# Long attention on one Trainium2 core: weighted sum in full fp32 on two column halves of TensorE, row sums by additions

## The chip, the cores and the metric

One core of a Trainium2 chip runs the whole program; the other seven are idle. The metric is the device time of one execution in microseconds. Three timed runs of the kernel before gave 3176.74, 3182.2 and 3185.15 us (median 3182.2).

Engines: PE is TensorE (matmuls; PEld is its load of the stationary operand), DVE is VectorE, ACT is ScalarE, POOL is GpSimd, and SP issues the DMAs.

## The reference

Four layers, each a cross attention of 896 queries (16 batches of 56) on a context, and a feed-forward part. The change touches the attention of layers 1, 2 and 3 ("long": 1500 keys per batch, 16 heads that share keys and values of width 64). With the weights folded, a batch computes for its 896 query rows (16 heads x 56)

```
scores = q @ k.T                     # 896 x 1500, contraction 64
attn   = softmax(scores, axis=-1)
ctx_c  = attn @ kv_rope              # 896 x 64, contraction 1500
out    = (fold of ctx_c over heads) @ B
```

`kv_rope` is the context with a rotary embedding, the same in the three layers. Layer 0 attends to the first 56 keys only ("short").

## The kernel before

**Precision.** An fp32r operand is read with reduced precision, in one pass of PE; an fp32 operand is multiplied in full. The kernel before splits both factors of each product into a high and a low fp32r part and adds three products (high x high, high x low, low x high).

**Short attention (`attend_short`, layer 0)** runs 8 steps of two batches and, beside it, `Rotation` makes the rotated context: `sines` on POOL, `cosines` and `sums` on DVE give `cr`; `value_highs` (ACT) and `value_lows` (DVE) split it into `vs`, which `store` writes to `kvn` in DRAM with extra columns (a column of ones at index 64, so that the weighted sum also gives the row sums). `turn`, `turned_highs` and `turned_lows` do the same for the transposed copy (`kvt_hi`, `kvt_lo`). Its DMAs are issued in order by SP: `load` of the next pair of batches, then `store` of an earlier one.

**Long attention (`attend_long`)** takes the 16 batches in turn. All engines run a program order written out by hand, unrolled over four batches. A batch has 12 units. A unit is two chunks of 125 keys against one half of the query rows (448 of 896): units 0 to 5 are the first query half, 6 to 11 the second.

- PE, per unit u: `scores` of unit u+2 (4 matmuls of 448 columns into banks 0 to 3, L1013); a `top_scores` piece (L1026, one matmul of 500 columns for the row maxima of the next batches, banks 6 and 7 in turns; 21 pieces per batch); `weigh_high` of unit u (4 matmuls, L1043: stationary `v` of 125 x 66, high and low part, moving `hi`); a second top piece; `weigh_low` (2 matmuls, L1050). They gather in bank 4 (first half) or 5 (second half). At u=7 `turn` (L1031) transposes the maxima. Units 0 to 6 and 8 to 10 have two pieces, unit 11 one, unit 7 none.
- ACT, per unit: two exponentials of the same scores, one to `raw` in fp32 (L1136), one to `hi` in fp32r (L1139).
- DVE, per unit: `tops` (L1083, the maximum of each piece) and `low` (L1095: `raw` minus `hi`).
- The row sums come as row 64 of the weighted sum. ACT copies it with the numerators (`cu`, L1145); SP sends it to DRAM and back across 128 partitions (`sums`), DVE inverts it (L1100), SP sends it to DRAM and back as 64 equal rows (`scales`), and POOL multiplies (`place`, L1184).
- SP, per batch: wait for the end of the last batch, then the loads of `qm`, `kl`, `v` (from `kvn`, 125 partitions x 6336 bytes) for the next batch, of `kh` and `q` for the one after, a wait until these have landed, `sums`, `shifts`, `scales`.

`project_out` (L1210) and the folding of weights (`fold_latent`, L414 and L432; `rotated_queries` of layer 2, L588 and L601) are not touched; they matter here because they multiply in full fp32. L1210 and L432 fill all 128 columns of PE. L414 and L601 use 64: L414 writes in turns to partitions 0 to 63 and 64 to 127 of a bank, L601 writes four records in a row to the same half. One full fp32 matmul is two MATMUL records in the trace.

Of the kernel before, what the change touches and what calls it, by code (L numbers as in the profile page):

```python
# [13 lines left out]
FP32 = mybir.dt.float32  # L14
# [23 lines left out]
DV = D + 2  # L38
HH = NH // 2
UNITS = 12  # L40
# [110 lines left out]
class Rotation:  # L151
# [6 lines left out]
    def __init__(self, G, st):  # L158
# [4 lines left out]
        self.vs = st.sb("vs", [KP, 2, NC, 2, DV], F32R)  # L163
        self.hi, self.lo = st.sb("hi", [128, L], F32R), st.sb("lo", [128, L], F32R)
        self.out_n, self.out_t = G["kvn_out"], G["kvt_out"]
        self.extra, self.tables = st.sem("extra"), st.sem("tables")
        self.in_n = [st.sem(f"in_n{u}") for u in range(2)]
        self.sin_n, self.cos_n, self.sum_n, self.hi_n, self.lo_n, self.turned, self.hi_t, self.lo_t = (
            st.sem(n) for n in ("sin_n", "cos_n", "sum_n", "hi_n", "lo_n", "turned", "hi_t", "lo_t"))
# [11 lines left out]
    def store(self, sp, m):  # L181
        sp.wait_ge(self.lo_n, m + 1)
        sp.dma_start(self.G["kvn"][bass.ds(m * 2, 2)].rearrange("b p n -> p b n"),
                     self.vs[:].rearrange("p b c h d -> p b (c h d)").bitcast(FP32)).then_inc(self.out_n, 16)
# [5 lines left out]
    def extra_columns(self, pool):  # L190

        parts = self.vs[:, :, :, :, :].rearrange("p b c h d -> p (b c) h d").bitcast(FP32)
        pool.memset(parts[:, :, 0, D:D + 1], 1.0).then_inc(self.extra, 1)
        pool.memset(parts[:, :, 0, D + 1:DV], 0.0).then_inc(self.extra, 1)
        pool.memset(parts[:, :, 1, D:DV], 0.0).then_inc(self.extra, 1)

# [12 lines left out]
    def sums(self, dve, m, u, first):  # L209

        dve.wait_ge(self.cos_n, m + 1)
        if not first:
            dve.wait_ge(self.turned, 3 * m)
        cn, cm = (v.rearrange("p b (c e d) -> p c b e d", e=2, d=D // 2) for v in (self.cn[:, u], self.cm[:]))
# [3 lines left out]

    def value_highs(self, act, m, first):
        if first:  # L220
            act.wait_ge(self.extra, 3)
        else:
            act.wait_ge(self.out_n, 16 * m)
        act.wait_ge(self.sum_n, 2 * m + 2)
        act.activation(self.vs[:, :, :, 0, 0:D], self.cr[:].rearrange("p c b d -> p b c d"),
                       ACT.Copy).then_inc(self.hi_n, 1)

    def value_lows(self, dve, m):
        dve.wait_ge(self.hi_n, m + 1)
        dve.tensor_tensor(self.vs[:, :, :, 1, 0:D], self.cr[:].rearrange("p c b d -> p b c d"),  # L230
                          self.vs[:, :, :, 0, 0:D].bitcast(FP32), ALU.subtract).then_inc(self.lo_n, 1)
# [428 lines left out]
def attend_short(nc, G, q_all, ctxT):  # L660
# [6 lines left out]
    with Stage(nc, "att0") as st:  # L667
# [22 lines left out]
        with nc.Block() as block:  # L690

            @block.sync
            def _(sp):
# [4 lines left out]
                def step(i, m, u, first, fresh):  # L698
                    rot.load(sp, m, u, fresh)
                    if not fresh:  # L700
                        rot.store(sp, m - 2)

                pairs(sp, step)
                for u in range(2):
                    rot.store(sp, LAST - 1 + u)
# [60 lines left out]
            def _(dve):  # L766
# [3 lines left out]
                def step(i, m, u, first, fresh):  # L770
# [11 lines left out]
                    if not first:  # L782
                        rot.value_lows(dve, m - 1)
# [22 lines left out]
                rot.value_lows(dve, LAST)  # L806
# [4 lines left out]
            def _(act):  # L811
                def step(i, m, u, first, fresh):
# [16 lines left out]
                    rot.value_highs(act, m, first)  # L829
# [6 lines left out]
            def _(pool):  # L836
                pool.memset(oc[:, :, NT, :], 0.0).then_inc(pad_done, 1)
                pool.memset(pw[:, :, NT * S:], 0.0).then_inc(pad_done, 1)
                rot.extra_columns(pool)
# [34 lines left out]
def attend_long(nc, G, l, ctxT):  # L874
# [5 lines left out]

    PS = G["PS"]
    with Stage(nc, f"att{l}") as st:
        kh, kl = st.sb("kh", [128, 4, L], F32R), st.sb("kl", [D + 1, 2, L], F32R)
        v = st.sb("v", [KP, 2, NC, 2, DV], F32R)
        q, qm = st.sb("q", [128, 4, NH * S], F32R), st.sb("qm", [D + 1, 2, NH * S], F32R)
        raw = st.sb("raw", [KP, 3, 2, HALF])
        hi, lo = st.sb("hi", [KP, 3, 2, HALF], F32R), st.sb("lo", [KP, 3, 2, HALF], F32R)
        top, nm = st.sb("top", [128, 2, NT, NS]), st.sb("nm", [128, 2, NT])
        nmh = st.sb("nmh", [NT, 2, 128], F32R)
        cu, rsb = st.sb("cu", [D + 1, 4, HALF]), st.sb("rsb", [D, 2, T])  # L890
# [889 lines left out]
```

## Time and profile before

| | us |
|---|---|
| median of three runs | 3182.2 |
| profiled execution, its own time | 3180.73 |
| its span | 3178.9 |
| PE busy | 2781.7 (88%) |
| DVE busy | 1970.7 (62%) |
| ACT busy | 1531.7 (48%) |
| POOL busy | 470.6 (15%) |

The mean granted clock of TensorE is 0.886 of 2.4 GHz; a granted clock of 0.50 is its level of 1.2 GHz. Long attention takes three stretches of some 500 us each, with other stages between (about 682 to 1194, 1452 to 1961 and 2385 to 2884 us in the profile). A row of the page's part 5 has the line, engine, operation, output<-input, shapes and count, then busy us and mean ns of one, then idle us before it and who ended them. Matmuls are pipelined: a record lasts longer than the distance to the next, so it is distances between starts, and not lengths, that add up to time on PE.

### The profile page before, as it was taken

How to read it: one execution, taken by the hardware profiler on the slowest of the kernel's cores; microseconds unless marked ns; L12 is line 12 of the kernel's file. 1: busy time of each engine (PE TensorE's matmuls, PEld its weight loads, DVE VectorE, ACT ScalarE, POOL GpSimd, SP SyncE). 2: the span in 40 equal slices, each digit the busy share in tenths (PEclk: the TensorE clock that was granted, in tenths of full speed). 3: DMA queues.
4: the chain of work that ended last, by engine and by line, in shares of the span. 5: the costliest groups of instructions: out<-in, count | busy, mean ns of one | idle time of the engine just before them, and what ended most of it. 6: DMA issues, size and time to landing. Idle time of an engine off the chain costs nothing. (4 is left out here: it accounts for less than half of the span.)

```text
span 3178.9 us, 38552 instructions
## 1 busy us (share of the span) xinstructions
PE 2781.7 (88%) x12773; PEld 2205.7 (69%) x12773; DVE 1970.7 (62%) x3007; ACT 1531.7 (48%) x2192; POOL 470.6 (15%) x350
## 2 busy tenths in 40 slices
PE   6777299779999985997999998699879999995798
PEld 4676199747777764654777776599757777774698
DVE  3563244258888864566888883344347888873444
ACT  3332144237777761213777774344226677771343
POOL 0221033000101110350010111133100010110232
PEclk9556599769999996997999999799868999997899
DMA  1333144363434412013443430233443443420343
GB/s 42 117 152 124 36 110 117 109 169 76 100 86 105 100 40 94 17 54 105 106 95 87 108 92 12 72 118 118 131 141 82 96 98 85 108 61 8 106 117 94
DMA packets 108025, 293.22 MB, mean 92 GB/s; under 512 B 24025, under 2 KB 49577, under 8 KB 106588
## 3 DMA queue, kind: packets, MB, share of 16 engines
q1 hardware_dynamic: 107900, 291.62, 34.6%
q8 instruction: 70, 1.15, 0.2%
q14 instruction: 55, 0.45, 0.0%
HBM read 241.90 MB, written 49.51 MB: 92 GB/s over the span
## 5 line engine op out<-in xcount | busy, mean ns | idle before, releaser
L1083 DVE TENSOR_REDUCE att_top<-banks 128x1 f32<-128x500 f32 x1008 | 670.9, 674 | 223.1 <-PE banks L1026 217.7
L1095 DVE TENSOR_TENSOR att_lo<-att_raw,att_hi 125x896 fp32r<-125x896 f32 x576 | 648.2, 1125 | 51.0 <-ACT att_hi L1139 48.0
L1136 ACT ACTIVATE att_raw<-banks 125x896 f32<-125x896 f32 x576 | 527.7, 916 | 306.6 <-PE banks L1013 302.1
L1043 PE MATMUL banks<-att_hi,att_v 125*66 125x448 f32 x2304 | 564.8, 367 | 0.0
L1139 ACT ACTIVATE att_hi<-banks 125x896 fp32r<-125x896 f32 x576 | 525.8, 913 | 0.0
L1395 PE MATMUL banks<-moe_xs,moe_w 128*128 128x448 f32 x2040 | 446.7, 369 | 69.4 <-DVE moe_xs L1510 67.2
L1026 PE MATMUL banks<-att_kh,att_q 128*128 128x500 f32 x1008 | 420.0, 424 | 55.6 <-DMA att_q<-q_rows 46.2
L1395 PEld LDWEIGHTS banks<-moe_xs,moe_w 128*128 128x128 f32 x2040 | 387.3, 190 | 103.0 <-DVE moe_xs L1510 68.7
L1043 PEld LDWEIGHTS banks<-att_hi,att_v 125*66 125x66 f32 x2304 | 317.2, 138 | 137.2 <-issue 0.4
L1184 POOL TENSOR_TENSOR ctx_ctxT<-att_cu,att_rsb 64x448 f32<-64x448 f32 x96 | 142.7, 1486 | 1408.9 <-DMA att_rsb<-rs_rows 1405.1
L1013 PE MATMUL banks<-att_q,att_kh 128*125 128x448 f32 x1152 | 333.6, 371 | 1.0 <-ACT att_hi L1139 1.0
L1050 PE MATMUL banks<-att_lo,att_v 125*66 125x448 f32 x1152 | 332.9, 370 | 0.0
L1013 PE MATMUL banks<-att_qm,att_kl 65*125 65x448 f32 x1152 | 332.2, 369 | 0.0
L1478 POOL TENSOR_TENSOR moe_sc<-moe_sg,moe_cb 128x448 f32<-128x448 f32 x170 | 196.1, 1153 | 683.2 <-ACT moe_sg L1452 683.2
L1500 DVE TENSOR_TENSOR moe_hf<-banks,moe_sc 128x448 f32<-128x448 f32 x170 | 106.2, 625 | 306.4 <-POOL moe_sc L1478 306.4
L1026 PEld LDWEIGHTS banks<-att_kh,att_q 128*128 128x128 f32 x1008 | 197.8, 197 | 133.8 <-DMA att_q<-q_rows 47.7
L1013 PEld LDWEIGHTS banks<-att_q,att_kh 128*125 128x125 f32 x1152 | 217.5, 189 | 52.9 <-ACT att_hi L1139 2.8
L1408 PE MATMUL banks<-moe_h,moe_w 128*128 128x448 f32 x1020 | 234.2, 366 | 4.1 <-DVE moe_h L1505 4.1
L1013 PEld LDWEIGHTS banks<-att_qm,att_kl 65*125 65x125 f32 x1152 | 217.4, 189 | 21.9
L1408 PEld LDWEIGHTS banks<-moe_h,moe_w 128*128 128x128 f32 x1020 | 191.4, 188 | 20.2 <-DVE moe_h L1505 5.2
L1050 PEld LDWEIGHTS banks<-att_lo,att_v 125*66 125x66 f32 x1152 | 155.8, 138 | 67.9 <-issue 10.4
L1460 ACT ACTIVATE moe_h<-moe_hf 128x448 fp32r<-128x448 f32 x170 | 98.5, 580 | 195.0 <-DVE moe_hf L1500 195.0
(182 smaller groups left out, 2484.2 us busy)
## 6 DMA issues: line engine op xcount, KB each, us to landing
moe_cb<-comb_rows SPq DMA_DIRECT2D x85, 448.0 KB
att_v<-kvn SPq DMA_DIRECT2D x48, 773.4 KB
att_kh<-kvt_hi SPq DMA_DIRECT2D x96, 375.0 KB, 8.4
moe_raw<-L_experts_dram SPq DMA_DIRECT2D x85, 384.0 KB, 6.1
q_rows<-mats_q SPq DMA_DIRECT2D x24, 896.0 KB
att_q<-q_rows SPq DMA_DIRECT2D x48, 448.0 KB, 16.0
att_kl<-kvt_lo SPq DMA_DIRECT2D x48, 375.0 KB, 5.5
kvn<-att_vs SPq DMA_DIRECT2D x8, 1546.9 KB
```

Source lines behind the costliest of these rows:

```text
L1013: last = pe.matmul(PS[2 * (u % 2) + c % 2][0:KP, 0:HALF], k[:, KP * c:KP * c + KP], rhs[:, HALF * e:HALF * e + HALF], start=part == 0, sto ...
L1026: pe.matmul(PS[6 + (PIECES * s + n) % 2][:, 0:SB], q[:, s, 128 * t:128 * t + 128], kh[:, s, SB * c:SB * c + SB], start=True, stop=True).th ...
L1043: pe.matmul(PS[4 + e][0:DV, 0:HALF], v[:, s % 2, c, part, :], hi[:, u % 3, c % 2, :], start=c == part == 0, stop=False)
L1050: last = pe.matmul(PS[4 + e][0:DV, 0:HALF], v[:, s % 2, c, 0, :], lo[:, u % 3, c % 2, :], start=False, stop=c == NC - 1)
L1083: dve.tensor_reduce(top[:, s % 2, n // NS, n % NS:n % NS + 1], PS[6 + (PIECES * s + n) % 2][:, 0:SB], AX.X, ALU.max).then_inc(mx_done, 1)
L1095: dve.tensor_tensor(lo[:, u % 3], raw[:, u % 3], hi[:, u % 3].bitcast(FP32), ALU.subtract).then_inc(dve_low, 1)
L1136: act.activation(raw[:, u % 3], scored, ACT.Exp).then_inc(exp_done, 1)
L1139: act.activation(hi[:, u % 3], scored, ACT.Exp).then_inc(hi_done, 1)
L1184: pool.tensor_tensor(ctxT[64 * e:64 * e + 64, :, b * S:b * S + S], a, r, ALU.mult).then_inc(placed, 1)
L1395: last = pe.matmul(PS[2 * e + m][:, 0:HALF], w[:, s, pw, o:o + 128], xs[:, px, k, HALF * e:HALF * e + HALF], start=n == 0, stop=n == 3 * K ...
L1408: last = pe.matmul(PS[4 + 2 * d + e][:, 0:HALF], w[:, s, pw, o:o + 128], h[:, s, ph, e, :], start=start and n == 0, stop=stop and n == 2)
L1478: pool.tensor_tensor(sc[:, e, :], sg[:, e, :], cb[:, s, HALF * e:HALF * e + HALF], ALU.mult).then_inc(comb_done, 1)
```

## The change

- Values are kept whole: `Rotation` stores `cr` itself to `kvn` (`store_values`, 64 floats per key, no extra columns, runs of 256 bytes); `value_highs`, `value_lows` and the memsets go. `sums` now waits for the store of the step before. In `attend_long`, `v` is 125 partitions x 3072 bytes.
- A unit is one chunk of 125 keys against both query halves. Its four `scores` matmuls are the same in number and size.
- ACT makes one exponential per unit, in fp32, into a ring of four (`ex`).
- `weigh` replaces `weigh_high` and `weigh_low`: two full fp32 matmuls per unit, stationary `v` of 125 x 64, the first query half into partitions 0 to 63 of a bank, the second into 64 to 127.
- Row sums: DVE adds two units (`pair`, six per batch), POOL adds the pairs up (`gather`, five per batch of 125 x 896), and at unit 3 of the next batch PE multiplies the result by a column of ones: 7 full fp32 matmuls (`sums`) with a stationary operand of 128 columns that lie 7 floats apart, into the bank of the top pieces. DVE inverts from PSUM. The top piece number 13, the next in that bank, waits for the inverse.
- SP has no `sums` any more; `scales` goes ahead of `shifts` and loads two halves of 64 partitions. `place` is one multiplication of 128 x 448.

```diff
@@ PE
-                def weigh_high(s, b, u): ...   # 4 matmuls fp32r, v 66 columns, moving hi
-                def weigh_low(s, b, u): ...    # 2 matmuls fp32r, moving lo
+                def weigh(s, b, u):
+                    pe.wait_ge(exp_done, UNITS * b + u + 1)
...
+                    for e in range(2):
+                        last = pe.matmul(PS[4 + s % 2][64 * e:64 * e + 64, 0:HALF], v[:, s % 2, u, :],
+                                         ex[:, u % RING, e, :], start=u == 0, stop=u == UNITS - 1)
+                    last.then_inc(pv_done, 1)
+                def sums(s, b, tops):
+                    pe.wait_ge(gathered, GATHERS * b + GATHERS)
+                    pe.wait_ge(mx_done, tops)
+                    for t in range(NT):
+                        last = pe.matmul(sums_bank(s)[:, t:t + 1], acc[:, (s + 1) % 2, t:T:NT], one[:, :],
+                                         start=True, stop=True)
+                    last.then_inc(sums_ready, 1)
@@ top_scores
+                    if n == SUMS_PIECE and not known(b, 2):
+                        pe.wait_ge(inverted, b - 1)
@@ batch on PE, unit u
+                        if u == SUMS_AT and not known(b, 1):
+                            sums(s, b - 1, PIECES * b + PIECES + (SUMS_PIECE - 1 if left else 0))
@@ DVE
-                def low(b, u): ...
+                def pair(b, p):
+                    dve.wait_ge(exp_done, UNITS * b + 2 * p + 2)
...
+                    dve.tensor_tensor(two[:, p % 3, :], ex[:, a].rearrange("p e n -> p (e n)"),
+                                      ex[:, a + 1].rearrange("p e n -> p (e n)"), ALU.add).then_inc(paired, 1)
@@ ACT
+                        act.wait_ge(pv_done, UNITS * b + u - RING + 1)
+                        act.wait_ge(paired, PAIRS * b + (u - RING) // 2 + 1)
...
+                    act.activation(ex[:, u % RING], scored, ACT.Exp).then_inc(exp_done, 1)
@@ POOL
+                    pool.tensor_tensor(a, two[:, 0, :] if n == 1 else a, two[:, n % 3, :], ALU.add).then_inc(gathered, 1)
...
+                    pool.tensor_tensor(ctxT[:, :, b * S:b * S + S], c, r, ALU.mult).then_inc(placed, 1)
@@ Rotation
+    def store_values(self, sp, m):
+        sp.wait_ge(self.sum_n, 2 * m + 2)
+        sp.dma_start(self.G["kvn"][bass.ds(m * 2, 2)].rearrange("b p (c d) -> p c b d", c=NC), self.cr[:]
+                     ).then_inc(self.out_n, 16)
```

## Rows read from the trace of the kernel before

**Rows 1.** The page's part 5, three groups of long attention (columns above).

```profile
L1083 DVE TENSOR_REDUCE att_top<-banks 128x1 f32<-128x500 f32 x1008 | 670.9, 674 | 223.1 <-PE banks L1026 217.7
L1095 DVE TENSOR_TENSOR att_lo<-att_raw,att_hi 125x896 fp32r<-125x896 f32 x576 | 648.2, 1125 | 51.0 <-ACT att_hi L1139 48.0
L1136 ACT ACTIVATE att_raw<-banks 125x896 f32<-125x896 f32 x576 | 527.7, 916 | 306.6 <-PE banks L1013 302.1
```

**Rows 2.** Windows of two batches: length, each engine's busy us (records), clock, DMA.

```profile
756.60:786.40 29.80, 29.80 (x144) 22.80 (x143) 25.98 (x36) 21.64 (x28) 3.04 (x2) 1.00 0.41 92
2502.00:2535.40 33.40, 31.64 (x145) 23.72 (x144) 26.29 (x36) 21.68 (x29) 2.83 (x2) 0.95 0.40 92
```

**Rows 3.** Timeline of PE, units 7 and 8 of a batch: start, length, what.

```profile
849.18 0.97 PE L1043 MATMUL banks<-att_hi,att_v 125*66 125x448 f32 x4
850.08 0.38 PE L1031 MATMUL banks<-ident,att_nm 128*7 128x128 f32 x2
850.39 0.62 PE L1050 MATMUL banks<-att_lo,att_v 125*66 125x448 f32 x2
850.85 0.58 PE L1013 MATMUL banks<-att_q,att_kh 128*125 128x448 f32 x2
...
853.35 0.57 PE L1013 MATMUL banks<-att_q,att_kh 128*125 128x448 f32 x2
```

**Rows 4.** Timeline of PE, queries of layer 2 (64 columns, one half).

```profile
1307.14 1.72 PE L601 MATMUL banks<-q_tc,mats_N 96*64 96x448 f32 x4
1308.79 2.68 PE L588 MATMUL banks<-q_xs,mats_Q 128*96 128x448 f32 x12
1311.39 1.72 PE L601 MATMUL banks<-q_tc,mats_N 96*64 96x448 f32 x4
```

**Rows 5.** Timeline of DVE, folding: copies, each after four heads of L414.

```profile
616.46 0.69 DVE L472 COPY keep_B<-banks 128x512 f32<-128x512 f32 x1 [0.17 <-PE banks L414]
617.33 0.69 DVE L472 COPY keep_B<-banks 128x512 f32<-128x512 f32 x1 [0.17 <-PE banks L414]
```

**Rows 6.** Windows of L414, L1210 and L432 alone: length, PE (records), PEld, clock, DMA.

```profile
615.37:617.10 1.73, 1.73 (x18) 0.98 (x14) 1.00 0.00 0
1200.05:1206.05 6.00, 6.00 (x29) 5.29 (x28) 1.00 0.00 0
617.30:619.00 1.70, 1.70 (x16) 1.70 (x17) 1.00 0.00 0
```

**Rows 7.** Timeline: a handover from DVE to PE.

```profile
701.98 0.67 DVE L1083 TENSOR_REDUCE att_top<-banks 128x1 f32<-128x500 f32 x1
702.70 0.28 PEld L1026 LDWEIGHTS banks<-att_kh,att_q 128*128 128x128 f32 x1 [0.30 <-DVE att_top L1083]
```

**Rows 8.** Timelines of ACT, DVE and POOL: end of layer 3's attention.

```profile
2870.74 0.54 ACT L1145 ACTIVATE att_cu<-banks 65x448 f32<-65x448 f32 x1 [1.92 <-PE banks L1050]
2876.43 0.20 DVE L1100 RECIPROCAL att_rout<-att_rin 128x7 f32<-128x7 f32 x1 [6.31 <-DMA att_rin<-rs_rows]
2881.42 2.32 POOL L1184 TENSOR_TENSOR ctx_ctxT<-att_cu,att_rsb 64x448 f32<-64x448 f32 x2 [4.05 <-DMA att_rsb<-rs_rows]
```

**Rows 9.** One line's durations, ns: min/median/max.

```profile
L1095 DVE TENSOR_TENSOR att_lo<-att_raw,att_hi x576: 1073/1081/2067, 709.4 to 2868.9; 125x896 fp32r<-125x896 f32 x192
L1184 POOL TENSOR_TENSOR ctx_ctxT<-att_cu,att_rsb x96: 1120/1157/2030, 774.9 to 2882.6; 64x448 f32<-64x448 f32 x96
L657 POOL TENSOR_TENSOR q_tc<-q_tc,q_ts x32: 2072/2117/2123, 1304.6 to 1432.9; 96x896 f32<-96x896 f32 x32
```

**Rows 10.** Timeline of SP, two steps of short attention.

```profile
179.83 0.58 SPq L178 DMA_DIRECT2D att_cn<-ctxN_dram  x1
...
205.75 0.36 SPq L178 DMA_DIRECT2D att_cn<-ctxN_dram  x1
```

**Rows 11.** Windows while `kvn` is stored, and while `q_rows` is (896-byte runs).

```profile
191.00:202.00 11.00, 11.00 (x53) 10.88 (x54) 2.17 (x4) 0.83 (x2) 0.00 (x0) 0.50 0.32 130
651.00:673.00 22.00, 16.91 (x46) 8.20 (x44) 16.19 (x26) 12.94 (x25) 0.00 (x0) 0.93 0.97 311
```

More of the change, by code:

```diff
@@ L699, in step @@
                     rot.load(sp, m, u, fresh)
+                    if not first:
+                        rot.store_values(sp, m - 1)
                     if not fresh:
-                        rot.store(sp, m - 2)
+                        rot.store_turned(sp, m - 2)
                 pairs(sp, step)
+                rot.store_values(sp, LAST)
                 for u in range(2):
-                    rot.store(sp, LAST - 1 + u)
+                    rot.store_turned(sp, LAST - 1 + u)
             @block.tensor
@@ L992, in _ @@
                     if b:
-                        sums(b - 1)
+                        scales(b - 1)
                     if b < B - 1:
                         shifts(b + 1)
-                    if b:
-                        scales(b - 1)
-                sums(B - 1)
                 scales(B - 1)
@@ L1010, in scores @@
                             pe.wait_ge(m_in[s % 2], of_two(s, b, 16))
-                        for c in (2 * j, 2 * j + 1):
+                        for e in range(2):
                             k, rhs = (kh[:, s, :], q[:, s, :]) if part == 0 else (kl[:, s % 2, :], qm[:, s % 2, :])
-                            last = pe.matmul(PS[2 * (u % 2) + c % 2][0:KP, 0:HALF], k[:, KP * c:KP * c + KP],
+                            last = pe.matmul(PS[2 * (u % 2) + e][0:KP, 0:HALF], k[:, KP * u:KP * u + KP],
                                              rhs[:, HALF * e:HALF * e + HALF], start=part == 0, stop=part == 1)
@@ L1076, in _ @@
                 scores(0, 0, 1)
+                pe.wait_ge(ones, 2)
                 emit(pe, batch)
+                pe.wait_ge(inverted, B - 1)
+                sums(0, B - 1, PIECES * B)
             @block.vector
@@ L1114, in batch @@
                             shift((s + 1) % 4, b + 1)
-                        if u == 10 and not known(b, 1):
-                            invert(s + 1, b - 1)
                 for n in range(PIECES):
@@ L1174, in _, with gather @@
                 pool.memset(kl[D:D + 1, :, :].bitcast(FP32), 1.0).then_inc(ones, 1)
+                pool.wait_ge(ones, 1)
+                pool.memset(one[:, :], 1.0).then_inc(ones, 1)
+                def gather(b, n):
+                    a = acc[:, b % 2, :]
+                    pool.wait_ge(paired, PAIRS * b + n + 1)
+                    if n == 1 and b >= 2:
+                        pool.wait_ge(sums_ready, b - 1)
+                    if n > 1:
+                        pool.wait_ge(gathered, GATHERS * b + n - 1)
+                    pool.tensor_tensor(a, two[:, 0, :] if n == 1 else a, two[:, n % 3, :], ALU.add).then_inc(gathered, 1)
                 def place(b):
                     s = b % 2
[L1180 to L1189 removed]
+                    pool.wait_ge(rs_in[s], b // 2 * 32 + 32)
+                    pool.wait_ge(cu_done, b + 1)
+                    c, r = (m[:, s, :].rearrange("p (h s) -> p h s", s=S) for m in (cu, rsb))
+                    pool.tensor_tensor(ctxT[:, :, b * S:b * S + S], c, r, ALU.mult).then_inc(placed, 1)
+                pool.wait_ge(ones, 2)
+                for b in range(B):
+                    for n in range(1, PAIRS):
+                        gather(b, n)
+                        if n == 3 and b:
+                            place(b - 1)
+                place(B - 1)
 def project_out(nc, G, l, Bm, ctxT):
```

179 lines of the change are left out of this document (59 added, 120 removed).

## The prediction, made blind

> **What bounds the kernel now.** I read the page's shares first, then windows of single batches of long attention, then the timeline of PE inside one batch, and last the few places elsewhere in the trace where full fp32 matmuls run. The page has PE at 88% of the span. In a batch of long attention it is everything: 29.80 us of 29.80 at granted clock 1.00 (2.4 GHz), while DVE has 25.98, ACT 21.64 and POOL 3.04 [rows 2]. So long attention, 48 batches of 29.8 us or 1430 of 3179 us, is a queue of PE records, and the change has to be judged by the length of that queue. DVE is the second: a top piece costs 0.67 and a `low` 1.13 us, 576 of them; one exponential costs ACT 0.92 [rows 1]. A unit with two top pieces takes 2.50 us (850.85 to 853.35) [rows 3].
>
> A batch holds 120 fp32r records of 448 columns, 21 of 500 and the turn. The turn adds 0.45 us: from 849.18 to 850.85 there are four records of L1043, the turn and two of L1050 in 1.67 us, six at 0.204 make 1.22 [rows 3]. 29.35 us over 64,260 columns are 0.457 ns per column, so 0.205 us for a record of 448.
>
> **The weighted sum.** Removed are six records per unit: 1.23 us. Added are two full fp32 matmuls, which are four records. Their pace without halves: L1210 runs 28 to 29 records of 256 columns in 6.00 us at clock 1.00, 0.21 us each or 0.84 ns per column, and a matmul is two [rows 6]. With 448 columns a record takes 0.376 us. If the four ran one after another they would take 1.50 us and the change would lose. The halves decide.
>
> L414 shows them. It alternates between partitions 0 to 63 and 64 to 127; a copy on DVE waits for each four heads, that is for eight records of 256 columns. Two such waits end 0.87 us apart (616.46 and 617.33, DVE idle and waiting for PE both times) [rows 5], at granted clock 1.00 [rows 6]. That is 0.108 us per record, half of L1210's. Its order, two records for one half and then two for the other, is the new unit's. So a unit's four records fill two slots: 2 x 0.376 = 0.75 us.
>
> What PE pays to go from full-width records to 64-column ones and back: L601 (64 columns, 448 moving, four records, all to one half, so no overlap) starts at 1307.14, and the next full-width record at 1308.79: 1.65 us against 4 x 0.376 = 1.50, so 0.15 more. The twelve L588 records after it take 2.60 against 12 x 0.205 = 2.46, 0.14 more [rows 4]. A round trip is 0.29 us. The turn gives a lower value: L1031 starts 0.08 late, L1050 0.09 after its two records of 128 columns (0.22) should have ended, and the next 0.05 late, 0.22 us in all [rows 3]. I take 0.29, since L601 has the new records' shape; 0.22 is the lower bound, and 0.34 the upper (0.05 more, if the second half's first load also shows). The new unit spends 0.75 + 0.29 = 1.04 us in place of 1.23: 0.19 saved, times 576 = **-107 us** (-147 to -78).
>
> **Row sums on PE.** 7 matmuls, 14 records with one moving column, so their load of 128 stationary columns sets the pace. L432 (128 columns, 64 moving) runs 15 to 16 records in 1.70 us at clock 1.00: 0.11 us each [rows 6]. 14 x 0.11 = 1.54 us, 48 times = **+74 us**. No record of before has a stationary operand with a step of 7 floats; bounds are 0.106 (the same row) and 0.21 (half its pace), so +71 to +141. A gain is excluded: PE has no idle time in a batch to hide them [rows 2].
>
> **The wait for the inverse.** After `sums` the order has top piece 13, which waits for DVE. What PE loses: the last record's end lies about 0.16 after the next one could start (500-column top pieces last 0.39 and follow at 0.23; I take the difference), a handover of 0.05 (DVE ends at 702.65, PE's load starts at 702.70) [rows 7] twice, the reciprocal 0.20 [rows 8]. 0.46 us, of which nothing is covered, because S, W and the rest stand behind the waiting piece on PE's queue; 45 batches (the last of each layer is in the tail): **+20 us** (+13 to +36, when DVE is still in a top piece).
>
> **Small terms.** The turn now follows a 64-column record and precedes a full one, so it shares that record's way back: 0.31 in place of 0.45, at most -6 us, I take **-3**. One batch took 33.40 us with PE idle 1.8 us and the clock at 0.95 [rows 2], waiting for the load of `q`; that load stands behind `v`, which falls from 6336 to 3072 bytes per partition. `v` uses few DMA engines, as the store of `kvn` from the same 125 partitions does (share 0.32, 130 GB/s) [rows 11], so this stall goes: **-4** (0 to -6).
>
> **DVE, ACT, POOL in a batch.** DVE has two top pieces per unit and one `pair` per two units: 21 x 0.67 + 6 x 1.1 = 20.7 of 29 us, was 26. ACT 12 x 0.92 + 0.5 = 11.5. POOL five adds of 125 x 896, 2.12 us each by L657, and one multiplication of 448, 1.16: 12 us [rows 9]. None is near PE. `gather` follows its `pair` at once and the next `pair` is two units, 4.6 us, later, so they hardly meet. The last `gather` ends some 4 us after unit 11 starts, `sums` comes 9 us after. SP's `scales` moves ahead of `shifts`: it takes over the 2 to 3 us in which `sums` waited for its DMA, and the row that scores of the next batch need at unit 10 is as early as before. Cost: nothing.
>
> **Tails.** Before, from the last weighted sum (2870.74) to the end of `place` (2881.42 + 2.32): 13.0 us [rows 8]. Now `pair` and `gather` follow the last exponential, so `sums` starts about 1.4 us after the last `weigh`; then 0.2, from the reciprocal to `place` 4.99 [rows 8], `place` 1.16 [rows 9]: 7.8 without `sums` (counted above). 5.2 saved, three times: **-16 us** (-8 to -20).
>
> **Short attention.** A step takes 25.9 us (179.83 to 205.75) [rows 10]. What goes on ACT and DVE (3.6 us per step) lies beside PE and stays hidden: zero, at best -5. The store of `kvn` moves to the front of the queue and ahead of the next load, with 3000 runs of 256 bytes. Its bytes are half (768 KB at 130 GB/s: 6 us); if each run costs what a run of 896 bytes costs (311 GB/s over 16 engines: 0.046 us) and it too uses 5 engines, 600 x 0.046 = 28 us [rows 11]. The two copies of `kvt` and the load behind it need some 10 us more (2.25 MB, at the two rates of rows 11). Below 16 us the step is not touched; at 28 it grows by 12, seven times: +84. I take a run at 0.024, 14 us, and **+3** (-5 to +84).
>
> The Trainium skill (SBUF — State Buffer, the part on Door 1: the DMA port swizzle) says that SBUF is read in lines of 16 bytes and that each access that crosses to a new line pays; with a step of 28 bytes every column of `sums` does. No row here shows such a load, and the rows on L432 have contiguous columns. By the rule the price is that of the first rival below.
>
> **Sum.** -107 + 74 + 20 - 3 - 4 - 16 + 3 = -33 from the profiled execution's own 3180.7 us: 3148; that execution is 1.5 us under the median of the runs, so **3149 us**.
>
> **Rivals.** (A) *The strided load halves the pace of `sums`.* 0.21 in place of 0.11 per record, 14 x 48 times: +67, 3216 us, slower than before. It decides from 0.16 per record on (-33 + 34). For: every load in the trace that keeps 0.11 is contiguous. Against: nothing in the trace. (B) *The halves don't overlap in so short a burst.* Between two full-width records four records might need three slots: +0.376 x 576 = +217, 3366 us. Against: L414's groups show two slots per two matmuls, but in a run of 16. (C) *The short runs stretch short attention:* +72 more than I took, 3220 us. (D) *Smaller passage and quick handovers:* 0.22 per round trip and 0.3 us per wait, -40 and -7: 3102 us. (E) *Collisions of DVE and POOL:* L1095 has a maximum of 2067 ns against a median of 1081, L1184 2030 against 1157 [rows 9], so an operation doubles when the two meet. If each `pair` met a `gather`, two units would take DVE 4 x 0.67 + 2.07 = 4.75 us against PE's 4.63: +0.12, five times per batch, 48 batches: +29, 3178 us, no change.
>
> **Chances.** Forecast 0.53, A 0.14, B 0.04, C 0.08, D 0.14, E 0.07. The forecast's own range is 3115 to 3185 (the passage -40 to +29, the wait -7 to +16, the rest within 10). A measurement of this kernel tells about 0.3%, 9.5 us, from no change: faster is below 3172.7, slower above 3191.7. Of the forecast's 0.53 I put 0.47 below, 0.05 within and 0.01 above; D is faster, E within; A splits 0.02 below, 0.02 within, 0.10 above, C 0.02 below, 0.01 within, 0.05 above, B above. Faster 0.65, same 0.15, slower 0.20. The range that holds 8 in 10 is 3105 to 3230.
>
> **What would show it.** Right: in a batch of the changed kernel PE is still busy all the time at clock 1.00, a batch takes about 29.5 us (29.8 - 2.3 + 1.5 + 0.5 - 0.1); the four records of `weigh` start within 0.38 us (two slots), and `scores` behind them 1.04 us after the first; `sums` takes 1.5 us and one gap of 0.5 follows; the tail is near 9.3 us. Wrong: `weigh` records one by one at 0.376; `sums` near 3 us; DVE or POOL named as what PE waits for; steps of short attention above 26 us, waiting for `kvn`.

## The result, and the profile after

The changed kernel takes 3377.3 us (median of 4 runs, 3372.09 to 3386.32), the kernel before, run beside it, 3179.5: ratio 1.063 with a 95% interval of [1.0611, 1.0649], so 6.3% slower. The forecast was 3149 us with a range of 3105 to 3230. The profiled execution has a span of 3373.4 us and a mean granted clock of 0.845, where before had 3178.9 and 0.886.

Lines have moved: L1083 is now L1060 (top pieces on DVE), L1136 is L1115 (exponential), L1026 is L999 (top pieces on PE), L1013 is L984 (`scores`), L1184 is L1168 (`place`). L1014 is `weigh`, L1023 the row sums, L1075 `pair`, L1161 `gather`, L1082 the reciprocal. From the page's shares and its part 5:

```profile
PE 2971.3 (88%) x12293; PEld 2014.0 (60%) x12293; DVE 1685.5 (50%) x2711; ACT 1041.4 (31%) x1560; POOL 889.5 (26%) x542
...
L1060 DVE TENSOR_REDUCE att_top<-banks 128x1 f32<-128x500 f32 x1008 | 679.5, 677 | 524.9 <-PE banks L999 510.0
L1115 ACT ACTIVATE att_ex<-banks 125x896 f32<-125x896 f32 x576 | 528.2, 917 | 1058.8 <-PE banks L984 1058.8
L1161 POOL TENSOR_TENSOR att_acc<-att_acc,att_two 125x896 f32<-125x896 f32 x192 | 405.4, 2111 | 537.6 <-DVE att_two L1075 537.1
L1075 DVE TENSOR_TENSOR att_two<-att_ex 125x896 f32<-125x896 f32 x288 | 320.9, 1116 | 60.7 <-ACT att_ex L1115 60.0
```

DVE, ACT and POOL did what the prediction said: the operations of before kept their length (L1060 677 ns against 674 [rows 1]), DVE and ACT got lighter, and both wait for PE longer. PE's busy time grew by 190 us (2781.7 to 2971.3). So the loss is on PE. Its timeline in units 2 and 3 of a batch (start, length, engine, line, what, count, idle before):

```profile
851.60 0.97 PE L1014 MATMUL banks<-att_ex,att_v 125*64 125x448 f32 x4
852.50 0.49 PE L999 MATMUL banks<-att_kh,att_q 128*128 128x500 f32 x1
852.84 0.57 PE L984 MATMUL banks<-att_q,att_kh 128*125 128x448 f32 x2
853.25 0.57 PE L984 MATMUL banks<-att_qm,att_kl 65*125 65x448 f32 x2
853.66 3.18 PE L1023 MATMUL banks<-att_one,att_acc 125*128 125x1 f32 x14
857.34 0.47 PE L999 MATMUL banks<-att_kh,att_q 128*128 128x500 f32 x1 [0.50 <-DVE att_rout L1082]
857.74 0.97 PE L1014 MATMUL banks<-att_ex,att_v 125*64 125x448 f32 x4
858.64 0.79 PE L999 MATMUL banks<-att_kh,att_q 128*128 128x500 f32 x1
859.22 0.95 PE L984 MATMUL banks<-att_q,att_kh 128*125 128x448 f32 x2
```

Two things are to be seen. From the first record of the row sums (853.66) to top piece 13 (857.34) PE spends 3.68 us; the prediction had 1.54 + 0.46 = 2.0. And from 858.6 the same instructions take longer: two records of `scores` last 0.95 us where they lasted 0.57 six us earlier. The windows say why (length, PE busy and records, PEld, DVE, ACT, POOL, granted clock, DMA share, GB/s); the first two are whole batches, the third the stretch of the row sums, the fourth what follows:

```profile
801.86:835.16 33.30, 32.91 (x135) 18.46 (x134) 20.34 (x29) 11.71 (x14) 11.61 (x6) 0.95 0.34 74
835.16:870.06 34.90, 34.40 (x134) 19.33 (x133) 20.29 (x29) 11.71 (x14) 11.60 (x6) 0.90 0.32 71
851.20:857.30 6.10, 5.64 (x26) 4.42 (x24) 1.97 (x4) 1.83 (x2) 0.00 (x0) 1.00 0.90 173
857.30:864.10 6.80, 6.76 (x18) 3.51 (x19) 3.30 (x5) 0.92 (x1) 2.09 (x1) 0.60 0.16 50
```

Behind each stretch of row sums the granted clock falls from 1.00 to 0.50 (2.4 to 1.2 GHz) for 3.4 to 10.2 us; such a time at 0.50 is called a fall here. Counted in each layer from 35 us behind the first weighted sum to the last, the kernel before was at 0.50 for 3.4 us in the three layers together, the changed one for 304. Of 42 batches 26 last 33.3 us (3.4 us at 0.50), three 34.4 to 34.9 and 13 35.8 us (10.2 us at 0.50), in place of 29.8 [rows 2].

### The profile page after: what moved, and what is told of

It reads as the page before. It is cut to its first block and busy times, and to the rows that moved or that the text cites. A ratio compares the mean times of both kernels' runs of the same rounds, so it can differ in the third digit from the quotient of the medians.

```text
span 3373.4 us, 36689 instructions
## 1 busy us (share of the span) xinstructions
PE 2971.3 (88%) x12293; PEld 2014.0 (60%) x12293; DVE 1685.5 (50%) x2711; ACT 1041.4 (31%) x1560; POOL 889.5 (26%) x542
## 5 line engine op out<-in xcount | busy, mean ns | idle before, releaser
L1060 DVE TENSOR_REDUCE att_top<-banks 128x1 f32<-128x500 f32 x1008 | 679.5, 677 | 524.9 <-PE banks L999 510.0
L1115 ACT ACTIVATE att_ex<-banks 125x896 f32<-125x896 f32 x576 | 528.2, 917 | 1058.8 <-PE banks L984 1058.8
L1014 PE MATMUL banks<-att_ex,att_v 125*64 125x448 f32 x2304 | 614.5, 615 | 0.0
L999 PE MATMUL banks<-att_kh,att_q 128*128 128x500 f32 x1008 | 496.2, 500 | 70.8 <-DMA att_q<-q_rows 42.7
L1161 POOL TENSOR_TENSOR att_acc<-att_acc,att_two 125x896 f32<-125x896 f32 x192 | 405.4, 2111 | 537.6 <-DVE att_two L1075 537.1
L999 PEld LDWEIGHTS banks<-att_kh,att_q 128*128 128x128 f32 x1008 | 211.2, 210 | 463.3 <-DVE att_top L1060 384.5
L984 PE MATMUL banks<-att_q,att_kh 128*125 128x448 f32 x1152 | 373.1, 408 | 0.0
L984 PE MATMUL banks<-att_qm,att_kl 65*125 65x448 f32 x1152 | 357.7, 394 | 0.0
L1075 DVE TENSOR_TENSOR att_two<-att_ex 125x896 f32<-125x896 f32 x288 | 320.9, 1116 | 60.7 <-ACT att_ex L1115 60.0
L984 PEld LDWEIGHTS banks<-att_q,att_kh 128*125 128x125 f32 x1152 | 226.6, 206 | 99.6 <-ACT att_ex L1115 42.1
L1161 POOL TENSOR_TENSOR att_acc<-att_two 125x896 f32<-125x896 f32 x48 | 102.7, 2140 | 620.5 <-DVE att_two L1075 620.5
L984 PEld LDWEIGHTS banks<-att_qm,att_kl 65*125 65x125 f32 x1152 | 238.0, 207 | 25.8
L1014 PEld LDWEIGHTS banks<-att_ex,att_v 125*64 125x64 f32 x2304 | 122.3, 144 | 202.9 <-issue 202.6
L1395 PEld LDWEIGHTS banks<-moe_h,moe_w 128*128 128x128 f32 x1020 | 191.4, 188 | 20.3 <-DVE moe_h L1492 5.2
L1023 PEld LDWEIGHTS banks<-att_one,att_acc 125*128 125x128 f32 x672 | 158.4, 324 | 6.2 <-issue 5.5
L1023 PE MATMUL banks<-att_one,att_acc 125*128 125x1 f32 x672 | 153.2, 356 | 2.9 <-issue 2.9
```

The source lines that it names most:

```text
L984: last = pe.matmul(PS[2 * (u % 2) + e][0:KP, 0:HALF], k[:, KP * u:KP * u + KP], rhs[:, HALF * e:HALF * e + HALF], start=part == 0, stop=pa ...
L999: pe.matmul(PS[6 + (PIECES * s + n) % 2][:, 0:SB], q[:, s, 128 * t:128 * t + 128], kh[:, s, SB * c:SB * c + SB], start=True, stop=True).th ...
L1014: last = pe.matmul(PS[4 + s % 2][64 * e:64 * e + 64, 0:HALF], v[:, s % 2, u, :], ex[:, u % RING, e, :], start=u == 0, stop=u == UNITS - 1)
L1023: last = pe.matmul(sums_bank(s)[:, t:t + 1], acc[:, (s + 1) % 2, t:T:NT], one[:, :], start=True, stop=True)
L1060: dve.tensor_reduce(top[:, s % 2, n // NS, n % NS:n % NS + 1], PS[6 + (PIECES * s + n) % 2][:, 0:SB], AX.X, ALU.max).then_inc(mx_done, 1)
L1075: dve.tensor_tensor(two[:, p % 3, :], ex[:, a].rearrange("p e n -> p (e n)"), ex[:, a + 1].rearrange("p e n -> p (e n)"), ALU.add).then_in ...
```

## The experiments

A batch is measured as the distance between two of DVE's L1065 reductions (one per batch, the shift); the first of the 15 distances of a layer is left out, so there are 42. Each ratio is taken to runs of the kernel before that were made beside the kernel; their medians were 3172.6 to 3181.1 us. A batch counts in the last column if some of it is at 0.50. Where a text written ahead of a run speaks of 14 one-column matmuls, these are the 14 records of seven matmuls.

| kernel | median us | ratio to before, 95% | batch at clock 1.00 | batches with falls |
|---|---|---|---|---|
| after | 3377.3 | 1.063 [1.0611, 1.0649] | none seen | 42 of 42 |
| e1_together | 3225.7 | 1.0151 [1.0117, 1.0186] | 30.24 | 19 |
| e2_wide_moving | 3306.6 | 1.0399 [1.0367, 1.0432] | 31.88 | 28 |
| e3_no_row_sums | 3076.8 | 0.9677 [0.9651, 0.9704] | 28.09 | 0 |
| e4_other_bank | 3371.3 | 1.0611 [1.0581, 1.064] | 31.22 (one) | 41 |
| e5_ones_stationary | 3122.7 | 0.9826 [0.9813, 0.984] | 28.83 | 0 |
| e6_together_other_bank | 3168.5 | 0.9972 [0.996, 0.9985] | 29.64 | 4 |
| e7_values_between | 3073.0 | 0.9669 [0.9654, 0.9684] | 28.09 | 0 |
| e8_same_half | 3504.7 | 1.1034 [1.1017, 1.1051] | 37.03 | 0 |
| e9_spread | 3490.4 | 1.0972 [1.0948, 1.0996] | none steady | 39 |
| e10_standing | 3356.9 | 1.0564 [1.0547, 1.0581] | none | 42 |
| e12_spread_shifts_first | 3205.3 | 1.0105 [1.0084, 1.0126] | 30.58 | 0 |
| e11_both | 3112.5 | 0.9795 [0.978, 0.981] | 28.82 | 1 |

A fall of 3.4 us costs a batch 1.5 us (e1_together: medians 30.24, 31.79 and 33.24 us with none, one and two times 3.4 us at 0.50). The experiments e3_no_row_sums, e7_values_between, e8_same_half and e10_standing leave out row sums, and e1_together and e6_together_other_bank mix them up: only their time counts.

**e1_together: contiguous loads.** `sums` takes `acc[:, (s + 1) % 2, 128 * t:128 * t + 128]` in place of `t:T:NT`, so each row is divided by another row's sum.

> The changed kernel, but each of the seven row-sum matmuls loads 128 columns that lie together in place of 128 with a step of 7 floats; so each query row is divided by another row's sum (left wrong: only the time counts). Stride theory: the records of the row sums follow at 0.11 us as contiguous fp32 loads do, not 0.23, so 14 x 0.12 = 1.7 us less per batch, -80 us. Rival (the pace comes from the form with one moving column, whatever the step): 0.23 stays, no change, 3377 us. On the clock: if the granted clock falls because PE stands in the row sums too long, the stretch is now 2.4 us in place of 4.1 and the low stretches (about 100 us per layer) shrink; then up to another 95 us go, 3200 us. If it falls for another reason, about 3295 us.

The records of L1023 now start 0.112 us apart (median), in after 0.230. From the first to the next top piece it is 2.10 us, at its end a wait for the inverse:

```profile
877.91 1.62 PE L1023 MATMUL banks<-att_one,att_acc 125*128 125x1 f32 x14
880.01 0.46 PE L999 MATMUL banks<-att_kh,att_q 128*128 128x500 f32 x1 [0.48 <-DVE att_rout L1082]
```

The price of the predicted term, 2.0 us, holds for contiguous columns; the stride of 28 bytes adds 1.6 us per batch. And of 42 batches with falls 19 are left.

**e2_wide_moving: 64 ones instead of one.** `one` is [KP, 64] and each matmul writes 64 equal columns.

> The changed kernel, but the moving operand of the row-sum matmuls is 64 equal columns of ones in place of one; DVE inverts every 64th. Result as before. Step, number of records and the wait for the inverse stay. Clock theory (the granted clock falls in every batch because PE moves almost no columns during the row sums): the low stretches go or shrink, a batch loses up to 2 us, 3377 - 95 = 3282 us, with the records still at 0.23 us. Rival (the clock falls because of the wait after the row sums, or by itself in this mix of half-width and full-width records): low stretches as before, 3377 us.

The pace stays 0.231, so the load sets it and not the moving side. Fourteen batches are undisturbed: 31.88 us is about the price of after's own instructions at clock 1.00 (from the first row-sum record to piece 13 it is 3.73 us here, 3.67 in after). The theory holds in part and its rival doesn't: with 64 moving columns per record, in a stretch as long as that of after, 28 of 42 batches have a fall in place of all, and the time is 71 us less than that of after, where the theory had up to 95. So what streams in the stretch matters for the clock.

```profile
868.28:900.16 31.88, 31.40 (x136) 17.72 (x135) 20.36 (x30) 11.71 (x14) 11.63 (x6) 1.00 0.35 78
900.16:933.62 33.46, 32.97 (x136) 18.49 (x135) 20.45 (x30) 11.71 (x14) 11.60 (x6) 0.95 0.35 75
```

**e3_no_row_sums.** No row sums on PE and no wait for them; DVE inverts other numbers, so the division is by wrong values.

> The changed kernel without the row sums on PE and without the top piece's wait for the inverse (left out: the sum over keys; DVE inverts seven other numbers). Additions on DVE and POOL, the DMAs and the multiplication stay. My account of the weighted sum: a unit takes 2.37 us in place of 2.50, so 12 x 0.13 = 1.6 us less than before per batch, 48 batches -77, tails -20, short attention +9: 3091 us, clock 1.00 throughout long attention. If the half-width records by themselves made the clock fall, low stretches would stay and it would be near 3190 us. If POOL or DVE were what PE waits for, a wait of theirs would stand in the trace and it would be over 3150 us.

Row sums, wait and clock together are 3377 - 3077 = 300 us of the changed kernel; the prediction had 94. There is no fall, so the 64-column records alone don't bring the clock down, and PE has no idle time in a batch, so it waits for neither DVE nor POOL. The total is 14 us below the expected 3091. A batch without them:

```profile
853.86:881.96 28.10, 28.10 (x121) 14.41 (x120) 20.26 (x30) 11.71 (x14) 11.61 (x6) 1.00 0.42 88
```

**e4_other_bank: no wait behind the row sums.** They go to the free weigh bank, and top piece 13 doesn't wait (in its place the first `weigh` of the next batch waits for an inverse made long before):

```diff
-            return PS[6 + (PIECES * (s + 1) + SUMS_PIECE) % 2]
+            return PS[4 + (s + 1) % 2]
@@ top_scores
-                    if n == SUMS_PIECE and not known(b, 2):
-                        pe.wait_ge(inverted, b - 1)
```

> The changed kernel, but the row sums go to the bank of the weighted sum of the batch before, which ACT has copied by then, so no top piece waits for the inverse. Result as before; step and number of records stay. Wait theory: 0.7 us of PE's wait per batch go, -34 us, 3343 us, with the clock falling as before. Rival (the clock falls only because the wait comes on top of the row sums): the low stretches go too, 3377 - 34 - 95 = 3248 us.

The wait went and next to nothing was gained: 3371 us where 3343 was expected. The next full record follows 0.23 us behind the last row-sum record (in after 0.85), but the clock is down sooner and for 6.8 us in 37 batches of 42:

```profile
852.96 3.18 PE L1022 MATMUL banks<-att_one,att_acc 125*128 125x1 f32 x14
856.00 0.77 PE L997 MATMUL banks<-att_kh,att_q 128*128 128x500 f32 x1
856.69 1.76 PE L1013 MATMUL banks<-att_ex,att_v 125*64 125x448 f32 x4
```

So the clock falls without the wait too. Its single batch without a fall takes 31.22 us.

**e6_together_other_bank** is e1_together and e4_other_bank in one.

> e1_together and e4_other_bank in one: contiguous loads for the 14 one-column matmuls, and sums in a free weigh bank, so that no top piece waits for the inverse. Theory (the clock falls because of the stretch of one-column matmuls, with or without the wait behind it): at full clock 30.24 - 0.52 = 29.7 us per batch, and falls go on in at least half of the batches: about 3225.7 - 25 = 3200 us or more. Rival (in e1_together the wait of 0.74 us behind the short matmuls made the clock fall): no falls, 29.7 us per batch: 3225.7 - 25 - 45 = 3155 us.

```profile
870.05 1.62 PE L1022 MATMUL banks<-att_one,att_acc 125*128 125x1 f32 x14
871.54 0.47 PE L997 MATMUL banks<-att_kh,att_q 128*128 128x500 f32 x1
```

My theory of that moment failed: with the stretch cut to 1.49 us (no stride, no wait) only 4 batches of 42 have a fall, and the time is 3168 us where it said 3200 or more. The same 14 one-column records, contiguous in both, had 19 with the wait behind them (2.10 us). So it is not enough that one-column matmuls are there; the length of what stands between two full-width streams counts, be it records or the wait.

**e10_standing: the same stretch without the matmuls.** Only the first of the seven is run; DVE then computes 440 unused reciprocals, and seven of other numbers, before it releases PE:

```diff
-                    for t in range(NT):
+                    for t in range(1):
@@ DVE, invert
-                    dve.reciprocal(rout[:, (s + 1) % 2, :], sums_bank(s)[:, 0:NT]).then_inc(inverted, 1)
+                    dve.reciprocal(slow[:, (s + 1) % 2, :], acc[:, (s + 1) % 2, 0:440])
+                    dve.reciprocal(rout[0:KP, (s + 1) % 2, :], acc[:, (s + 1) % 2, 0:NT]).then_inc(inverted, 1)
```

> From after: of the seven row-sum matmuls of a batch only the first is run, and DVE inverts, ahead of the seven numbers, 440 more per partition (7.5 ns each by e5's 844 ns for 112, so 3.3 us) before it lets PE's next top piece go; the other rows' sums are left out. PE thus stands for some 3.5 to 3.7 us where after spends 2.8 us in one-column matmuls and 0.85 us in the wait. At full clock 28.09 + 0.35 + 3.6 = 32.0 us per batch. Theory (for the clock a stretch of one-column matmuls is as good as standing still: what matters is that no columns stream): it falls in every batch as in after, 33.5 us or more, 3345 us or more. Rival (the one-column matmuls themselves bring the clock down, standing still doesn't): no falls, 32.0 us per batch, 3265 us.

```profile
858.54 0.42 PE L1023 MATMUL banks<-att_one,att_acc 125*128 125x1 f32 x2
862.23 0.47 PE L999 MATMUL banks<-att_kh,att_q 128*128 128x500 f32 x1 [3.26 <-DVE att_rout L1083]
```

PE stands for 3.69 us from the first row-sum record (after: 3.68), and the batches come out the same to 0.1 us: 33.33 with one fall, 35.8 with three (after: 33.31 and 35.79). For the granted clock, 3.7 us of one-column matmuls are worth no more than standing still. The 20 us between the two medians lie in the last batch of each layer, which the 42 distances don't cover: it has no top piece left that would wait, so e10_standing doesn't stand there, while after still runs its 14 records and has falls behind them. From a layer's last shift to the end of `place` it is 45 us in e10_standing and 51 to 53 in after.

**e9_spread and e12_spread_shifts_first: the same matmuls, one per unit.** Seven in the units 3 to 9 of the next batch, in the free bank, still strided.

> From e4_other_bank: the seven row-sum matmuls (two records each, so 14 records 0.230 us apart) are not issued in one stretch in unit 3 but one in each of the units 3 to 9, each in front of the unit's first top piece; same number, same strided loads, same bank. Theory (the granted clock falls because PE spends some 3 us in one stretch on them): no falls, 31.2 to 31.4 us per batch as in the one undisturbed batch of e4 (31.22), 3371 - 48 x 2.8 = some 3235 us. Rival (their sum over a batch is what counts, wherever they stand): falls of 6.8 us per batch as in e4, 34.1 us per batch, 3371 us.

e9 missed its question. Its edit moved the inverse to unit 9, and SP, which sends the inverses ahead of the shifts, held the shifts back; PE waited 3.1 us per batch at the end:

```profile
PE banks L984 <- DMA att_qm<-att_nmh: 25.1, 8, 3.4
```

(eight batches; total, times, longest). At 3490 us it is the slowest but one, for a DMA order. e12 turns that order round and moves POOL's product with it:

```diff
+                    if b < B - 1:
+                        shifts(b + 1)
                     if b:
                         scales(b - 1)
-                    if b < B - 1:
-                        shifts(b + 1)
@@ POOL
-                        if n == 3 and b:
+                        if n == 5 and b:
```

> In e9_spread SP's transfer of the shifts stood behind the transfers of the inverted sums, which its edit had moved from unit 3 to unit 9, and PE stood 3.1 us per batch for it; that hid the answer. Here the spread row sums of e9 again (one matmul in each of the units 3 to 9), with SP's transfer of the shifts issued ahead of that of the inverted sums, and POOL's product after its last addition instead of its third. Theory (a stretch of some 3 us of one-column matmuls in one place lets the granted clock fall, the same matmuls spread don't): no falls, 12 units of 2.37 us and 7 x 0.38 us = 31.1 us per batch, 3371 - 48 x 3.0 = some 3225 us. Rival (their sum over a batch counts wherever they stand): 6.8 us of falls per batch as in e4, 34.1 us, 3371 us.

```profile
854.91:885.52 30.61, 30.61 (x136) 17.75 (x135) 20.34 (x29) 11.71 (x14) 11.60 (x6) 1.00 0.37 81
```

No batch of the 42 has a fall: as many strided one-column matmuls as in e4_other_bank, 166 us less. Of the mean 3.4 us less per batch (33.91 to 30.52) 0.6 is that the spread matmuls are cheaper at clock 1.00 (31.22 to 30.58), the rest are the falls.

**e8_same_half: what the two halves are worth.** From e3_no_row_sums; both halves of the queries are written to the same 64 partitions.

> From e3_no_row_sums: both query halves go to the same 64 columns of PE (and are added into the same 64 partitions, the other 64 rows of the output hold ones), so that nothing can overlap; the same number of matmuls and columns. Theory (in after the two halves run side by side): four slots of 0.43 us instead of two in each unit, +0.85 x 576 = +490 us, 3560 to 3580 us, if the clock stays. Rival (the records that start 7 ns apart only look so, the halves run one after the other in both): no change, 3077 us.

```profile
862.73 1.72 PE L1012 MATMUL banks<-att_ex,att_v 125*64 125x448 f32 x4
864.37 0.49 PE L997 MATMUL banks<-att_kh,att_q 128*128 128x500 f32 x1
```

1.64 us from `weigh` to the next full record, in after 0.90 (851.60 to 852.50). A unit grows by (37.03 - 28.09) / 12 = 0.745 us, two slots of 0.373 us: the overlap of the halves is real and complete, and worth 0.745 x 576 = 429 us. The expectation took slots of 0.43, which held the passage as well.

**e7_values_between: the order of three stores.** From e3_no_row_sums, at the end of `Rotation`:

```diff
-                rot.store_values(sp, LAST)
-                for u in range(2):
-                    rot.store_turned(sp, LAST - 1 + u)
+                rot.store_turned(sp, LAST - 1)
+                rot.store_values(sp, LAST)
+                rot.store_turned(sp, LAST)
```

> From e3_no_row_sums: at the end of the rotation of the keys and values in the short attention stage, the last two stores of turned keys and the last store of values in another order: turned, values, turned instead of values, turned, turned. Theory (the stage's 9 us more come from the store of the last highs and lows, which stands in the queue behind some 3000 short runs of the values): the last turn starts 6 to 8 us earlier, 3069 to 3071 us against 3076.8. Rival (the queue is emptied in the same time in any order, and the stage ends with it): no change, 3075 to 3078 us.

After's SP queue, then its ACT, and ACT of e7:

```profile
277.18 0.88 SPq L183 DMA_DIRECT2D kvn<-att_cr  x1
278.11 7.92 SPq L189 DMA_DIRECT2D kvt_hi<-att_hi  x1
286.08 0.42 SPq L190 DMA_DIRECT2D kvt_lo<-att_lo  x1
291.47 0.59 ACT L229 ACTIVATE att_hi<-banks 128x500 fp32r<-128x500 f32 x1 [11.79 <-DMA kvt_lo<-att_lo]
```

```profile
286.88 0.59 ACT L229 ACTIVATE att_hi<-banks 128x500 fp32r<-128x500 f32 x1 [3.83 <-DMA kvt_lo<-att_lo]
```

The DMA instruction right behind the 3000 short runs took 7.92 us to issue, where the same instruction took 0.33 behind another store (297.89). In the steps before it took 7.65 to 7.70 us each time, hidden beside PE. In the new order ACT waits 3.83 us instead of 11.81 (e3_no_row_sums). The stage itself, from the first PE record of the short attention to `project_out`, takes 221.8 us instead of 230.0 in the profiled executions, so the order is worth 8 us there; the medians of the whole program show only 3.8 of them, with intervals that overlap.

**e5_ones_stationary: the operands of the row sums swapped.** From after; the ones are loaded, the sums of exponentials stream, each half next to its own numerators:

```diff
...
+                    pe.wait_ge(cu_done, b + 1)
+                    for e in range(2):
+                        last = pe.matmul(PS[4 + (s + 1) % 2][64 * e:64 * e + 64, 0:HALF], one[:, :],
+                                         acc[:, (s + 1) % 2, HALF * e:HALF * e + HALF], start=True, stop=True)
@@ DVE, in four pieces in the units 4 to 7
+                    dve.reciprocal(rsb[:, (s + 1) % 2, w], PS[4 + (s + 1) % 2][:, w]).then_inc(inverted, 1)
```

> From after: the row sums of a batch are two full-width matmuls, one per query half, with 64 columns of ones as the stationary operand and the sums of exponentials as the moving one, right behind the weigh of unit 3, into the weigh bank of the batch before (copied out by then). Each half comes out on the 64 partitions where the product needs it, so the reciprocal is taken by DVE in four pieces of 112 columns from the bank, and the way of the reciprocals through DRAM is gone. Theory (the 14 one-column matmuls with their strided loads, their wait and the clock that falls behind them are the loss): against e3_no_row_sums (3076.8 us, 28.09 us per batch) a pair of halves more, two slots of 0.43 us, so 28.9 to 29.0 us per batch, granted clock 1.00 in all batches, 48 x 0.86 = +41 us, less some 10 us at the three ends of the attention for the way through DRAM: 3105 to 3120 us, below before (3181). Rival 1 (any work put into the batch beside the scores makes the clock fall): falls of 3.4 us in half of the batches as in e1_together, about +1 us per batch: 3155 to 3165 us. Rival 2 (DVE's reciprocals of 448 numbers per partition and batch hold up the maxima, 8 times the cost per element of a copy): 3 to 4 us of DVE per batch, of which what PE waits for shows in front of the top pieces: up to 3170 us.

```profile
871.02 0.97 PE L993 MATMUL banks<-att_ex,att_v 125*64 125x448 f32 x4
871.82 0.92 PE L1002 MATMUL banks<-att_acc,att_one 125*64 125x448 f32 x4
872.67 0.50 PE L977 MATMUL banks<-att_kh,att_q 128*128 128x500 f32 x1
```

```profile
L1061 DVE RECIPROCAL att_rsb<-banks 128x112 f32<-128x112 f32 x192 | 160.8, 844 | 20.7 <-PE banks L1002 20.7
```

The row sums cost 28.83 - 28.09 = 0.74 us per batch, two slots, in place of 3.8 and the falls: 1.7% faster than before, 255 us less than after. Rival 2 did not come: 3.4 us of reciprocals per batch fit beside PE (PE is busy all of a batch). The total is 3 us above the range expected.

**e11_both** is e5_ones_stationary with the store order of e7_values_between.

> e5_ones_stationary with the order of the stores of e7_values_between (turned, values, turned at the end of the rotation in the short attention): nothing of the two touches the other, so 8 us less at that place and 3122.7 less 4 to 8 = 3115 to 3119 us. Rival (the stage then ends with the last store all the same): 3120 to 3125 us.

3112.5 us, some 2% faster than before (ratio 0.978 to 0.981), and the fastest of the kernels that leave nothing out. The step from e5_ones_stationary is 10 us in the medians (0.9826 to 0.9795, intervals just apart) where 4 to 8 were expected; in the profiled executions the stage takes 221.6 us instead of 229.7, again 8 us.

Its one batch with a fall (35.15 us) is a case of its own: DVE stood for 4.64 us with nothing in the profile that it waited for, PE stood for DVE, and the records behind are at 0.50:

```profile
1690.48 0.79 PE L977 MATMUL banks<-att_kh,att_q 128*128 128x500 f32 x1 [3.81 <-DVE att_top L1038]
```

Once more it is PE standing that stands in front of a fall, here of 6.8 us. Why DVE stood stays open.

## Why the prediction was wrong

It was 228 us too low. Two steps failed: the price of the row-sum records (1), and the clock, which was taken as 1.00 throughout and had no term at all (2). By its own steps, with what the runs put in their place:

1. **Row sums on PE, +74 (bounds +71 to +141): failed, undersized.** The step took 0.11 us per record from L432 [rows 6], whose columns are contiguous. With a stride of 7 floats it is 0.230 (after), without it 0.112 (e1_together). 14 records and their edges: 3.04 us from the first record to the next full one where nothing is waited for (e4_other_bank), 1.49 without the stride (e6_together_other_bank). 48 times 3.04 are 146 us, 72 more than the step's 74 and outside its upper bound of 141; by the batches at clock 1.00 (31.22 against 28.09) it is 3.13 us, 76 more. This is rival A, to which I gave 0.14, and whose 0.21 per record was still 0.02 short. By the rule of the Trainium skill that the prediction quoted (SBUF — State Buffer, Door 1: the DMA port swizzle) the price was to be that of the rival; the pair e1_together and after agrees with it, 0.112 against 0.230 us for the same number of columns. The weights should have been the other way round: nothing in the trace spoke for 0.11 at such a stride.
2. **The clock: the term that was missing.** The prediction expected clock 1.00 throughout ("PE is still busy all the time at clock 1.00"). Over the 42 batches of after the mean is 34.2 us; at clock 1.00 a batch with row-sum records at the same pace takes 31.88 (e2_wide_moving). 2.3 x 48 = some 110 us (an estimate: the six stretches outside the 42 batches are taken as like those in them), the largest single part. The cause is shown by four kernels: it is the stretch of 3.7 us without wide streaming (e10_standing gives the same falls with PE standing) and its length (e6_together_other_bank: 4 batches with falls at 1.49 us, e1_together: 19 at 2.10), and not the number of such matmuls (e12_spread_shifts_first: none). The Trainium skill (TensorE: Matmul & The Clock Gate, Part 1) says that the clock is set by how busy PE has been recently; e10_standing agrees. What the prediction would have read as "busy" in the records of L1023 brought the same falls as no work at all.
3. **The wait for the inverse, +20: nearly right, but the wrong thing to price.** 0.85 us from the last record to piece 13, in e4_other_bank 0.23: 0.62 lost against 0.46. It is paid 42 times (the profile has 42 waits of L999 for the inverse) and not 45: 26 us, +6. Without falls it is worth 0.60 per batch (e1_together to e6_together_other_bank at clock 1.00, 30.24 to 29.64).
4. **Weighted sum, -107 (-147 to -78): right in its mechanism.** Two slots instead of four (e8_same_half). The passage was undersized: a unit takes 2.36 us (from one `weigh` at 849.24 to the next at 851.60), was 2.50 [rows 3], predicted 2.31. So `weigh` with its passage costs 1.23 - 0.14 = 1.09 us and not 1.04: with slots of 0.373 the round trip is some 0.34, the upper bound of the step, not 0.29: (2.364 - 2.31) x 576 = +31 us. Rival B is refuted.
5. **Short attention, +3: +9.** From its first PE record to `project_out` it grew from 221.2 to 230.3 us. The steps did not grow (rival C is out); the loss is the one wait at the end, which e7_values_between shortens by 8 us (221.8 us for the stage).
6. **Tails, -16: right.** From the last `weigh` of layer 3 (3066.9) to the end of `place` (3077.3) it is 10.4 us, 3.4 of it row sums: 7.0 without them, predicted 7.8, -2 us for three layers.
7. **DVE, ACT and POOL: right.** A batch has 20.3, 11.7 and 11.6 us of them; the prediction had 20.7, 11.5 and 12. Rival E's price did not come, but its collision is real. In the last batch of each layer, where no top pieces are left and the units are shorter, `pair` and `gather` meet and `pair` takes 3.07 us where its median is 1.08:

```profile
1215.92 3.07 DVE L1075 TENSOR_TENSOR att_two<-att_ex 125x896 f32<-125x896 f32 x1 [3.01 <-ACT att_ex L1115]
1215.92 2.12 POOL L1161 TENSOR_TENSOR att_acc<-att_acc,att_two 125x896 f32<-125x896 f32 x1
```

Only 6 of the 288 `pair` operations are stretched, two per layer, and PE waits for none of them.

72 to 76 for the row sums, + 110 + 6 + 31 + 6 - 2 = 223 to 227 of 228. The two small terms of the forecast (-3 for the turn, -4 for the stall of `q`) were not measured by themselves, and the clock term is good to some 10 us, so that the sum closes this well is partly luck. The first two terms are not independent: with contiguous loads the stretch is shorter and the falls are fewer, and the 152 us between after and e1_together hold both.

## What to carry to other kernels

When a tall block is summed over partitions by a product with ones, load the ones and stream the data: e5_ones_stationary paid 0.74 us where loading the data cost 3.8, it needed no trip through DRAM, and no fall of the clock came behind it in its 42 batches. A step that puts PE for some microseconds on loads with one moving column behind each must be priced like a stall of that length, with the slow stretch behind it in the sum, even where the page counts PE busy. And a price for a stationary operand is only worth the stride it was read at.

## What the runs showed of the hardware that I had not expected

- The records of the two 64-column halves start 7 ns apart (851.599 and 851.606, 852.026 and 852.033): the first record of each pair hides the other fully in a burst of four, between full-width records.
- In e4_other_bank removing a wait of 0.62 us per batch, 26 us in all, returned 6 us in the medians and 11 in the 42 batches (mean 34.18 to 33.91): the clock took the rest, 6.8 us at 0.50 in 37 batches where after has 3.4 in 26 and 10.2 in 13.
- DVE's reciprocal takes 844 ns for 112 columns from PSUM and 2.90 us for 440 from SBUF, 6.6 to 7.5 ns per column, against 205 ns for 7.
